# Logit sum, comparison results and rank sums of the expert choice in PSUM columns instead of SBUF tiles

## What is computed

```python
# x: (8, 256, 256); 16 heads of 128, rope part 64; a key is seen if qs-8 <= key index <= qs, index < 128
x = x + attention(layernorm(x), ctx, token ids, W_kvc, W_dq, W_uq, W_qr, W_uk, W_kr, W_uv, W_o)
h = layernorm(x)
gate_logits = h @ gate_w + gate_b                     # 8 experts
_, top_idx = top_k(gate_logits, 2)                    # ties: the lower index first
all_out = relu(einsum(h, expert_w) + expert_b)
x = x + mean of the two chosen experts' rows of all_out
```

## Time and profile before

| | us |
|---|---|
| median of 3 runs | 395.87 |
| lowest and highest run | 395.62, 397.86 |
| span of the profiled execution, first to last instruction | 391.2 |
| TensorE busy | 354.0 |
| VectorE busy | 288.3 |
| ScalarE busy | 264.0 |
| GpSimd busy | 234.1 |

### The profile page before, as it was taken

One profiled execution on the slowest core, in us unless ns is written; L12 is line 12 of the kernel. 1 busy time (PEld: TensorE's weight loads), 2 busy tenths in 40 slices (PEclk: granted clock), 3 DMA queues, 4 the chain that ended last, 5 costly groups with the idle time before them and its releaser, 6 DMA issues.

```text
span 391.2 us, 10358 instructions
## 1 busy us (share of the span) xinstructions
PE 354.0 (90%) x2507; PEld 289.2 (74%) x2507; DVE 288.3 (74%) x1395; ACT 264.0 (67%) x907; POOL 234.1 (60%) x326
## 2 busy tenths in 40 slices
PE   1989999998999999999999999999998788999940
PEld 0856877786688878888878888788886577888730
DVE  2367887788888889888788888888889566444455
ACT  1347777788878878778888788788787544445430
POOL 4616555468976777677677676776764355455500
PEclk9999999999999999999999999999999999999985
DMA  8964040000000000000000000000000354543178
GB/s 277 349 215 188 7 105 3 1 3 29 0 30 1 30 20 7 27 0 27 14 14 27 0 27 0 27 27 0 30 2 28 95 161 131 148 132 121 34 239 316
DMA packets 15093, 28.27 MB, mean 72 GB/s; under 512 B 2892, under 2 KB 10719, under 8 KB 14416
## 3 DMA queue, kind: packets, MB, share of 16 engines
q1 hardware_dynamic: 11408, 20.25, 16.1%
q0 software_dynamic: 2960, 6.94, 5.0%
q10 hardware_dynamic: 688, 0.64, 0.6%
HBM read 17.81 MB, written 10.91 MB: 73 GB/s over the span
## 4 chain that ended last, share of the span: by engine, by line
PE 65%; DVE 12%; issue 10%; POOL 7%; DMA 2%; ACT 2%; DVEq 0%; SPq 0%; POOLq 0%; ACTq 0%
PE psum L1133 11%; PE psum L672 8%; PE psum L673 8%; PE psum L674 8%; PE psum L1090 7%; PE psum L1203 6%; PE psum L1117 5%; POOL prob L1361 2%; DVE x_all L1554 2%; POOL q_sb L1347 2%; PE psum L1180 2%; DVE nsc L1622 2%; DMA wcat<-in_w_kvc 2%; PE psum L369 2%; PE psum L1012 1%
## 5 line engine op out<-in xcount | busy, mean ns | idle before, releaser
L1228 ACT ACTIVATE prob<-nsc,nmax 128x128 f32<-128x128 f32 x256 | 100.8, 396 | 36.3 <-DVE nmax L1622 35.5
L1347 POOL TENSOR_TENSOR q_sb<-rope_a,rope_b 128x256 f32<-128x256 f32 x64 | 47.5, 742 | 59.2 <-DVE rope_b L1585 55.1
L1361 POOL TENSOR_TENSOR prob<-prob,prec 128x512 f32<-128x512 f32 x64 | 67.2, 1050 | 7.4 <-DVE prec L1593 7.4
L1133 PE MATMUL psum<-kT_all,qT 128*128 (+1 forms) x512 | 68.6, 277 | 1.1 <-ACT qT L1271 1.1
L1622 DVE CUSTOM_DVE_ANT_0 nsc<-psum,mask 128x128 f32<-128x128 f32 x256 | 58.6, 284 | 13.0 <-PE psum L1133 13.0
L1133 PEld LDWEIGHTS psum<-kT_all,qT 128*128 128x128 f32 x512 | 62.1, 192 | 2.7 <-ACT qT L1271 2.4
L1415 POOL DMA_INDIRECT halves<-jout,jidx x33 | 32.2, 976 | 30.3 <-DVE jidx L1526 13.7
L1228 ACT ACTIVATION_READ_ACCUMULATOR prob<-nsc,nmax 128x1 f32 x256 | 48.4, 189 | 0.0
L1090 PE MATMUL psum<-ident,q_sb 128*128 128x128 f32 x256 | 41.9, 286 | 2.2 <-POOL q_sb L1347 1.8
L1090 PEld LDWEIGHTS psum<-ident,q_sb 128*128 128x128 f32 x256 | 26.8, 140 | 21.7 <-POOL q_sb L1347 13.6
L1203 PE MATMUL psum<-pT,v_cur 128*64 128x256 f32 x256 | 41.8, 405 | 0.0
(11 more groups left out here) (204 smaller groups left out, 878.1 us busy)
## 6 DMA issues: line engine op xcount, KB each, us to landing
wanted<-slots SPq DMA_DIRECT2D x33, 129.0 KB, 2.4
wo_raw<-in_w_o SPq DMA_DIRECT2D x2, 1024.0 KB, 14.9
we_raw<-in_expert_w SPq DMA_DIRECT2D x1, 2048.0 KB, 7.8
half<-halves SPq DMA_DIRECT2D x4, 512.0 KB, 7.1
x_all<-in_x SPq DMA_DIRECT2D x2, 640.0 KB, 17.4
slots<-pad_row SPq DMA_DIRECT2D x8, 129.0 KB, 3.4
we_raw<-in_ctx_near SPq DMA_DIRECT2D x1, 1024.0 KB, 11.2
out<-x_all SPq DMA_DIRECT2D x2, 512.0 KB, 4.6
```

What stands on the lines that cost most here:

```text
L1133: mm = pe.matmul(B_S[r][:, h, :], qT[r][:, h, :], batch_keys, start=True, stop=True)
L1228: e = act.activation(prob[r][:, h, :], nsc[r][:, h, :], ACT.Exp, bias=nmax[r][:, h:h + 1], scale=-1.0, accum_out=psum_h[r][:, h:h + 1])
L1347: pool.tensor_tensor(q_sb[1 - r][:, :, KVC:P], rope_a[1 - r][:], rope_b[1 - r][:], ALU.add).then_inc(m["rope_joined"], 1)
L1361: pool.tensor_tensor(p[:], p[:], prec[1 - r][:, :].unsqueeze(2).to_broadcast([P, HG, P]), ALU.mult).then_inc(m["prob_normed"], 1)
```

## The change

Four columns of eight numbers each, behind the rank products in bank 1, take the place of three SBUF tiles and of one use of two others: the sum of the logits (`both`), the two comparison results (`above`, `equal`) and the sum of ranks and filled rows (`place`). The count, the taken equal ones, the final choice and the product `taken` stay in SBUF. The threshold `top8` and `need` stay in SBUF too. Order, count and semaphores of the instructions are the same. In the program's other branch (for inputs whose ids go beyond the first 128 keys, not run with these inputs) the same columns of bank 7 are used.

```diff
+CHOICE = D + 4 * NE
...
-        place, taken = sb("place", [P, NE]), sb("taken", [P, NE])
+        taken = sb("taken", [P, NE])
...
-        eq2, eq_cum, eq_in, gt2 = sb("eq2", [P, NE]), sb("eq_cum", [P, NE]), sb("eq_in", [P, NE]), sb("gt2", [P, NE])
+        eq_cum, eq_in, gt2 = sb("eq_cum", [P, NE]), sb("eq_in", [P, NE]), sb("gt2", [P, NE])
...
+        place = B_E[:, CHOICE + 3 * NE:CHOICE + 4 * NE]
...
                 n = 6 * tile
+                both, above, equal = (z[:, CHOICE + NE * q:CHOICE + NE * q + NE] for q in range(3))
...
-                        dve.tensor_tensor(logit[:], logit[:], z[:, D + NE:D + 2 * NE], ALU.add).then_inc(m[step_sem], 1)
+                        dve.tensor_tensor(both, logit[:], z[:, D + NE:D + 2 * NE], ALU.add).then_inc(m[step_sem], 1)
...
-                        dve.max(top8[:], logit[:]).then_inc(m[step_sem], 1)
+                        dve.max(top8[:], both).then_inc(m[step_sem], 1)
...
-                        dve.tensor_scalar(gt2[:], logit[:], top8[:, 1:2], None, ALU.is_gt)
-                        dve.tensor_scalar(eq2[:], logit[:], top8[:, 1:2], None, ALU.is_equal).then_inc(m[step_sem], 1)
+                        dve.tensor_scalar(above, both, top8[:, 1:2], None, ALU.is_gt)
+                        dve.tensor_scalar(equal, both, top8[:, 1:2], None, ALU.is_equal).then_inc(m[step_sem], 1)
...
-                        dve.tensor_tensor_scan(eq_cum[:], ones8[:], eq2[:], 0.0, ALU.mult, ALU.add).then_inc(m[step_sem], 1)
+                        dve.tensor_tensor_scan(eq_cum[:], ones8[:], equal, 0.0, ALU.mult, ALU.add).then_inc(m[step_sem], 1)
...
-                        dve.scalar_tensor_tensor(out=eq_in[:], in0=eq_cum[:], scalar=need[:], in1=eq2[:],
+                        dve.scalar_tensor_tensor(out=eq_in[:], in0=eq_cum[:], scalar=need[:], in1=equal,
...
-                        dve.tensor_tensor(gt2[:], gt2[:], eq_in[:], ALU.add).then_inc(m[step_sem], 1)
+                        dve.tensor_tensor(gt2[:], above, eq_in[:], ALU.add).then_inc(m[step_sem], 1)
...
-                    dve.tensor_tensor(place[:], B_E[:, RANKS:RANKS + NE], filled[:], ALU.add).then_inc(m["place_step"], 1)
+                    dve.tensor_tensor(place, B_E[:, RANKS:RANKS + NE], filled[:], ALU.add).then_inc(m["place_step"], 1)
...
-                    dve.tensor_tensor(taken[:], place[:], gt2[:], ALU.mult).then_inc(m["place_step"], 1)
+                    dve.tensor_tensor(taken[:], place, gt2[:], ALU.mult).then_inc(m["place_step"], 1)
```

## The result

| | median us | ratio to before | 95% interval |
|---|---|---|---|
| before, beside it | 396.72 | | |
| after | 392.02 | 0.9896 | 0.987 to 0.9921 |

The change makes the kernel 1.04% faster by this measurement. Over all these executions the mean is 392.87 us for 33 of after and 395.99 us for 168 of before, so about -3.1 us. Three executions of before that took 611, 696 and 1184 us are left out of this. I had forecast -0.8. The range (393.8 to 396.9) holds neither 392.02 nor 392.87.

What follows compares the result with a forecast made beforehand. It took TensorE, busy 354.0 of the 391.2 us span, as the bound. 391.2 - 0.80 + 0.1 = 390.5 us, with 4.7 us around it 395.2, and a last 0.1 back gave 395.1 us; range 393.8 to 396.9.

Steps and rivals of the forecast that it cites:

- The hold and its end: Comparisons and the product with `place` no longer end with GpSimd's multiply; VectorE gets back some 14 us of 288.
- 75 to 108 us: Early stretch: the equality's 1.5 us stall passes to the residue of the expert weights; taken as 0, bound 2.05 us.
- The third rival: Early stretch pays too: L390 isn't held, TensorE's idle 2.05 us shrink, giving 394.1 or 393.0 us; chance 0.10.
- Tile 13: From 291.8 to 299.8 us: the held comparison goes, TensorE waits less for oT_lo; -0.80 us.
- The price of PSUM: Fourteen changed instructions on the path at 5 ns each: 0.1 us, ends 0 and 2.3 us.
- The first rival: The 14 instructions on the path: a PSUM operand costs more than it frees, up to 397.4 us; chance 0.17.
- the estimate of 65 ns: PSUM instead of SBUF costs 62 cycles more per instruction, 0.9 us for 14, making 396.0 us.
- the second rival: The hold stays or passes to the instruction after the choice, so the 0.80 us stay: 395.9 us; chance 0.13.
- The loop: From 108 to 274.3 us: TensorE's own queue covers VectorE's delay; taken as 0, bound 0.42 us.
- the sign of a wait I hadn't seen: The loop's period was to stay 33.2 us; a move would mean TensorE's queue hides a wait for VectorE.
- the 3.7 us of idle time: All TensorE idle time VectorE could give back in the stretches shown; faster by over 1% (4.0 us) got 0.02.
- The sum: Span 391.2 - 0.80 + 0.1 = 390.5 us, with 4.7 us around it 395.2; forecast 395.1 us.

Runs made afterwards that it cites:

- e4: The kernel after, but with the choice in PSUM only in tiles 13 to 15 (`place` in PSUM throughout): 395.07 us, 0.999 of before.
- e7: The kernel after, unchanged, measured again: 393.29 us, 0.9934 of before.
- d3: The kernel after, unchanged, since the transposes meant for slot 20 were not added: 0.9919 of before.
- e5: The kernel after, but with the choice in PSUM only in tiles 0 to 12 (`place` in PSUM throughout): 393.13 us, 0.9937 of before.
- e0: The kernel before, unchanged, measured again: 1.0002 of before.
- e2: The kernel before with only `place` moved to PSUM, the choice left in SBUF: 1.0009 of before.
- d2: The kernel before, unchanged, since the transposes meant for slot 20 were not added: 1.0005 of before.
- d4: The kernel before, unchanged, since the transposes meant for slot 20 were not added: 0.9997 of before.
- e1: The kernel before with only the choice moved to PSUM columns, `place` left in SBUF: 0.992 of before.
- e3: The kernel before with only the comparison results put into PSUM, the logits left in SBUF: 0.9914 of before.
- d1: The kernel after, unchanged, since the transposes meant for slot 20 were not added: 0.9922 of before.
- f2: The kernel after with 17 more transposes on TensorE in slot 58, behind the loop: 394.91 us, 0.9963 of before.
- g1: The kernel after with three added VectorE reductions of 128x256 ahead of the comparisons of tiles 2 to 12: 395.23 us, 0.999 of before.

## Why the prediction was wrong

- *The hold and its end.* Right: the comparisons are at 225 ns, the product at 167, the operand in PSUM takes them out of GpSimd's way. VectorE's busy time fell by 11.8 us and not 14, though the taken equal ones (L1457, 4.5 us in all, now 3.6) gave back 0.9 that I hadn't counted. Against that the rows show 1.0 more on L392 (below) and 0.3 on the two additions and the search for the largest values; the rest I haven't traced to a line.
- *75 to 108 us.* Right: the hold passed to the residue of the expert weights. Where the equality had been held for 1.71 us, L390 (now L392) went from 0.69 to 1.60 us, in after's timeline of VectorE and GpSimd:

```profile
96.25 1.06 POOL L1363 TENSOR_TENSOR prob<-prob,prec 128x512 f32<-128x512 f32 x1
...
96.12 0.22 DVE L1460 SCALAR_TENSOR_TENSOR eq_in<-eq_cum,need,psum 128x8 f32<-128x8 f32 x1
96.26 1.60 DVE L392 TENSOR_TENSOR we_lo<-we_raw,we_hi 128x512 fp32r<-128x512 f32 x1
```

  Slots 10 to 16 gained 0.11 us where I took 0. The third rival, with 1 us or more from here, did not come.
- *Tile 13.* Right: 0.80 forecast, 0.79 in the slots of the two traces, 0.88 in e4's. e4's median is 0.8 us lower as well, though not clear of the noise.
- *The price of PSUM.* 6 to 9 ns, inside the -4 to 11 that I had from the reads; the part behind slot 63 is 0.09 us longer in the pair of traces. That this is near the 0.1 of the sum is luck: the same kernel has 0.5 there in e7 and d3 (90.45 and 90.47 us against 89.97), so this part can't tell the price. The first rival, which decides from 57 ns, did not come. The same goes for the estimate of 65 ns from the Trainium skill ("VectorE: DVE Perf Modes", section on the TRN2 errata): between 128x8 in SBUF and in PSUM these traces have 6 to 9 ns. The scaling behind tile 13's choice isn't held either, so the second rival falls.
- *The loop.* This is the step that failed. I took 0, with 0.42 us, TensorE's idle time, as the bound. The loop's two-tile period went from 33.17 us (slots 34 to 42: 179.99 to 213.16) to 32.95 (180.77 to 213.72), which I had named as the sign of a wait I hadn't seen; it is worth 1.1 us. Two things were wrong in it. I looked at the transposes straight behind the choice, and there nothing waits; the wait comes four slots after the choice, where GpSimd, still 0.34 us late, has just issued its two indirect DMAs. And idle time is no bound here: the record of the group ahead overlaps the start of the next, so 0.1 us of waiting shows as busy. The 0.42 us counted only what was left over, and so did the 3.7 us of idle time from which I gave a gain of over 1% a chance of 0.02. With the loop's 1.1 us in it the sum would have been 394.0, still over the mean of 392.87: the rest of the miss is the part that stays open, below.
- *The sum.* My forecast used one execution's span and laid 4.7 us around it. Around every span with a time beside it lie 1.7 to 1.9 us. So the profiled execution took about 393.1 us, shorter than each of the 168 timed ones (lowest 393.67). The anchor on the median was safe, but the terms came from the shortest execution. That it has no fall before its end isn't what made it short, as the last paragraph of this section shows.

Of the 3.1 us, 0.1 + 1.1 + 0.8 = 2.0 stand in the slots, with their causes. About 1.1 do not. By the medians they go with the part in tiles 0 to 12 (e5: 2.7 against 1.2 in its slots). The fall in the tail was my candidate: it costs 1.1 to 1.4 us in e0, and it is in 4 of the 5 traces with the choice of before (before, e0, e2, d2, d4) and in 1 of the 6 with the loop and tile 13 freed (after, e1, e3, e7, d1, d3). But the record speaks against it. For every timed execution it has the mean granted clock, and each trace with a fall ahead of the one at the end has 0.983 or less. At 0.985 or more there are 44 executions of before, with a mean of 395.4 us (394.27 to 397.58), and 8 of after, with 391.9 (391.17 to 392.35). So executions that by this figure have no fall but the one at the end differ by 3.5 us, no less than all of them do. f2 and g1, made to settle it, disagree. What the 1.1 us are stays open.

## What to carry to other kernels

Idle time of the bounding engine is no bound on what a late feeder costs it: compare the start-to-start distance of its groups in a slot that waits for nothing with every other slot of the period, the ones behind DMA issues above all, and read the rows of its weight loads too. Follow a delay on one engine through the next engine's whole period, not to its first consumer. And before a sum is made on a profiled execution, see where it stands among the timed ones.

## What the runs showed of the hardware

- A PSUM output alone, with the input in SBUF, keeps a comparison from being held behind GpSimd's multiply (e3: 222 ns at most in 32 instances, against 1217 on L1452 before). The Trainium skill, "VectorE: DVE Perf Modes", section "Why PSUM operands drop a tier", says that any PSUM operand rules out the mode that takes both SBUF ports; "SBUF — State Buffer", section "Who interferes with whom", says that in this mode VectorE and GpSimd lock each other out for a whole instruction. These runs agree with both.
- A stall can pass from a freed VectorE instruction to the next one with two SBUF inputs: at the one place where the equality had been held for 1.71 us, L392 took 0.91 us more.
- The granted clock fell to 1.2 GHz for 3.4 us (once for 6.8, in e3) near 22 to 29 us in 14 of 20 traces, which costs 1.3 to 1.5 us between slots 0 and 1 (2.8 in e3), and between 324 and 329 us in 6 of 20 (1.1 to 1.4 us in e0), there after a stretch in which TensorE was busy 1.96 of 3.40 us. The same stretch without a fall, 1.99 of 3.40, is in before. One kernel has the fall in one execution and not in another (before and e0; after and d1).
